# Second half of the value projection moved between the two value-product runs, second half of the key transposes between the two score runs

## The reference

```python
qkv = x @ Wqkv                      # 128 -> 3 * 1024, 16 heads of 64
q = l2norm(q) * qs ; k = l2norm(k) * ksc      # then rotary tables on both
bq, bk, bv = windows of 32 tokens; keys and values of the window and of the one before it
sim = einsum('bhwie,bhwje->bhwij', bq, bk2) * 8
attn = softmax(where(mask, -max, sim))
out = einsum('bhwij,bhwje->bhwie', attn, bv2)
x = out @ Wo + x                    # then the feed-forward
```

## Time and profile before

| | |
|---|---|
| median of three executions | 3936.07 us |
| profiled execution | 3927.86 us, span 3926.1 us |
| TensorE matmul, busy | 94% of the span |
| TensorE weight load, VectorE, GpSimd, ScalarE, busy | 72%, 77%, 66%, 58% |
| mean granted TensorE clock | 0.988 |
| DMA | 48 GB/s mean |

### The profile page before, as it was taken

How to read it: one execution, slowest core, us unless ns; L and a number is a source line. 1 busy time by engine, 2 the same in 40 slices (tenths; PEclk the granted TensorE clock), 3 DMA queues, 4 the chain that set the end, 5 groups by cost and what they waited for, 6 DMA issues and landing times.

```text
span 3926.1 us, 163005 instructions
## 1 busy us (share of the span) xinstructions
PE 3686.9 (94%) x67712; PEld 2840.2 (72%) x67712; DVE 3008.4 (77%) x5061; ACT 2270.5 (58%) x4270; POOL 2597.5 (66%) x3029
## 2 busy tenths in 40 slices
PE   6999979999999999999999999999999999999998
PEld 3555547777767777668877677777677777778876
DVE  7666658878778788778887788877788887888876
ACT  3555546666546666456666466665466664566662
POOL 4545548777548787368887288775478874678870
PEclk8999989999999999999999999999999999999999
DMA  1000012222212222122222122222122221122220
GB/s 44 4 6 4 6 33 68 55 58 60 58 32 60 57 57 59 41 49 60 61 57 56 30 64 56 60 59 60 32 58 56 60 61 41 48 60 60 60 52 22
DMA packets 136307, 189.03 MB, mean 48 GB/s; under 512 B 38006, under 2 KB 58484, under 8 KB 135412
## 3 DMA queue, kind: packets, MB, share of 16 engines
q1 hardware_dynamic: 135540, 178.23, 17.7%
HBM read 22.67 MB, written 2.10 MB: 6 GB/s over the span
## 4 chain that ended last, share of the span: by engine, by line
PE 76%; issue 4%; POOL 3%; DVE 2%; ACT 0%; DMA 0%; POOLq 0%; SPq 0%; DVEq 0%; ACTq 0%
PE PS L1270 18%; PE PS L1417 10%; PE PS L1256 10%; PE PS L1294 8%; PE PS L1280 8%; PE PS L1257 8%; PE PS L1258 8%; PE PS L1476 2%; PE PS L1411 2%; PE PS L1454 1%; PE PS L1447 1%; POOL t L1182 1%; PE PS L1442 1%; POOL t L1187 1%; DVE m L1803 0%
## 5 line engine op out<-in xcount | busy, mean ns | idle before, releaser
L1182 POOL TENSOR_TENSOR t<-t 128x1024 f32<-128x1024 f32 x384 | 908.3, 2370 | 368.2 <-DVE t L1764 366.9
L1187 POOL TENSOR_TENSOR t<-t,rn 128x1024 f32<-128x1024 f32 x384 | 723.6, 1905 | 29.8 <-POOL rn L150 27.3
L1542 ACT ACTIVATE va<-PS 128x512 f32<-128x512 f32 x384 | 229.8, 598 | 631.9 <-PE PS L1258 631.6
L1763 DVE TENSOR_TENSOR t<-PS,rope 128x512 f32<-128x512 f32 x768 | 523.6, 682 | 27.9 <-ACT sq L1577 26.0
L1256 PE MATMUL PS<-w_hi,xh 128*128 128x512 f32 x1152 | 514.7, 447 | 22.8 <-DVE xl L1063 11.3
L1764 DVE TENSOR_TENSOR t<-PS,rope 128x512 f32<-128x512 f32 x768 | 522.9, 681 | 0.0
L1577 ACT ACTIVATE sq<-PS 128x512 f32<-128x512 f32 x768 | 454.2, 593 | 33.0 <-PE PS L1258 17.4
L1270 PE MATMUL PS<-constants,t 128*128 128x128 f32 x3072 | 443.3, 277 | 19.8 <-POOL t L1187 13.2
L1258 PE MATMUL PS<-w_lo,xh 128*128 128x512 f32 x1152 | 458.4, 398 | 0.0
L1257 PE MATMUL PS<-w_hi,xl 128*128 128x512 f32 x1152 | 458.3, 398 | 0.0
L1770 DVE TENSOR_REDUCE ss<-sq 128x16 f32<-128x1024 f32 x384 | 448.5, 1209 | 0.0
(11 more groups left out here) (167 smaller groups left out, 7697.7 us busy)
## 6 DMA issues: line engine op xcount, KB each, us to landing
vs<-va SPq DMA_DIRECT2D x768, 130.0 KB
vs<-va SPq DMA_DIRECT2D x768, 65.0 KB
t<-in_L_ffn_Wqkv SPq DMA_DIRECT2D x18, 512.0 KB, 4.5
w_out<-in_L_ffn_Wo SPq DMA_DIRECT2D x6, 512.0 KB, 3.9
a_normed<-in_L_attn_x SPq DMA_DIRECT2D x8, 256.0 KB, 6.4
a_xo<-in_L_attn_x SPq DMA_DIRECT2D x8, 256.0 KB, 2.9
out<-total SPq DMA_DIRECT2D x8, 256.0 KB, 3.5
w_raw<-in_L_ffn_W SPq DMA_DIRECT2D x6, 341.0 KB
```

The source lines that it names most:

```text
L1182: pool.tensor_tensor(mine[:, i, :], mine[:, i, :], t2[:, i, :], ALU.add).then_inc(done, 1)
L1187: pool.tensor_tensor(h, h, bc(rn[:, H * i:H * (i + 1)], 2, HB), ALU.mult).then_inc(done, 1)
L1763: dve.tensor_tensor(o1, src, bc(rope[:, 2 * i, t, :], 1, 8), ALU.mult)
```

## The change

On TensorE the second half of the value projection now stands between the two value-product runs, behind `turn_q(0)` alone, and goes to bank 5. Before it overwrites bank 5 it waits for the second rotary pair on the keys (`rk_made`). `turn_q(1)` goes behind the second value-product run and into bank 6, for which it waits for the rotary pair on q's first half (`rq_made`). `turn_mixed(1)` writes bank 5 and so waits for the value copy (`v_made`). The next slot's q projection into bank 6 waits for `qT_made` instead of `v_made`. `turn_k(1)` stands between the first score run and the output projection. On ScalarE the value copy goes between the two query copies. The closing slots keep `turn_q(1)` where it was. VectorE, GpSimd and SyncE have the same instructions in the same order.

```diff
+        def q_bank(projecting, c):
+            return 4 if c == 0 else 6 if projecting else 5
...
                 def turn_q(c):
                     pe.wait_ge(qn_made, at(T, 1, 1, 1))
                     if project_new:
-                        pe.wait_ge(rk_made, at(T, 0, 2, c + 1))
-                    turn(4 + c, lambda j: roped(0)(4 * c + j), qt_mm)
+                        if c == 0:
+                            pe.wait_ge(rk_made, at(T, 0, 2, 1))
+                        else:
+                            pe.wait_ge(rq_made, at(T, 0, 2, 1))
+                    turn(q_bank(project_new, c), lambda j: roped(0)(4 * c + j), qt_mm)
...
                 def turn_mixed(c):
                     if score:
                         pe.wait_ge(qT_made, at(T, 1, 2, c + 1))
+                    if project_new and c == 1:
+                        pe.wait_ge(v_made, at(T, 0, 2, 2))
...
                     project(1, 1, 5, t, k_mm)
-                    pe.wait_ge(v_made, at(T, 1, 2, 2))
+                    pe.wait_ge(qT_made, at(T, 2, 2, 2))
                     project(0, 0, 6, t, q_mm)
                 if closing:
-                    pe.wait_ge(v_made, at(T, 1, 2, 2))
+                    pe.wait_ge(qT_made, at(T, 2, 2, 2))
...
                 if score:
                     turn_q(0)
+                if closing:
                     turn_q(1)
+                if project_new:
+                    pe.wait_ge(rk_made, at(T, 0, 2, 2))
+                    project(2, 1, 5, t, v_mm)
                 if mix:
                     mix_half(1)
-                if project_new:
-                    pe.wait_ge(rq_made, at(T, 0, 2, 1))
-                    project(2, 1, 6, t, v_mm)
+                if score and not closing:
+                    turn_q(1)
...
                 if score:
-                    turn_k(1)
                     pe.wait_ge(on_made, at(T, 2, 2, 2))
...
                     score_half(0)
+                    turn_k(1)
...
                 def turned_q(c):
                     act.wait_ge(s_mm, at(T, 2, 1, 1))
                     act.wait_ge(qt_mm, at(T, 1, 2, c + 1))
-                    pairs(qT, c, 4 + c, qT_made)
+                    pairs(qT, c, q_bank(0 in ages, c), qT_made)
...
                     turned_q(0)
+                if 0 in ages:
+                    values(lay, s, t, 1, 5)
+                if 1 in ages:
                     turned_q(1)
-                if 0 in ages:
-                    values(lay, s, t, 1, 6)
-                if 1 in ages:
                     turned_k(0)
```

## The result

The changed kernel takes 3961.88 us in the median of six runs (3952.71 to 3966.03), against 3934.43 us for the kernel before in the same runs (3925.79 to 3943.39). The ratio is 1.0065, 95% interval 1.0046 to 1.0083. Repeated on another chip it was 1.0044 (1.0027 to 1.0062). It is slower, by 17 to 26 us, where 20 us less was forecast and 3952 us was the upper end of the range. The profiled execution took 3966.03 us; the one before took 3927.86 us.

A forecast was written before the change was run, and what follows sets the result against it. TensorE, busy 94% and 76% of the chain, was taken as the bound. Direct terms -26, -20.5 and +5 gave -41 us, the cautious reading -14; -20 was taken: 3936 - 20 = 3916 us, range 3892 to 3952.

The forecast's parts named there:

- a stop: In TensorE's small-matmul runs: end of a 16.4 KB instruction block whose successor has not landed; 1.10 us in one slot.
- (a): First to second value-product run: stretch grows from 1.02 to 1.33 us, winning 26 us, or 20 read cautiously.
- (b): First to second score run: stretch grows from 1.98 to 2.51 us, 3.30 us start to start, winning 20.5 us.
- cautious reading: Whole slot: loss interpolated against stretch length, winning 20 and 11 us, losing 17; sum -14 us.
- The rule behind the step: Between TensorE's runs: about 2.9 to 3.1 us must pass from start to start; a shortage is paid at block ends.
- (c): Second value-product run to first score run: stretch shrinks from 2.96 to 2.17 us, losing 5 us, bounds 0 and 67.
- Rival B: First score run becomes the new place of stops: +67 - 26 - 20.5 = +21 us, 3957 us; chance 0.18.
- Rival A: Stops only move to the first score run, transposes or output projection: 3936 us, 3925 to 3947; chance 0.29.
- (d): TensorE's new waits: keys' rotary pair has 1.0 us to spare, cover for `on` falls from 0.8 to 0.44 us.
- (e): ScalarE: value copy free; key copy ends 0.3 us before TensorE wants it; a sixth of a microsecond lost costs 30 us.
- C: Whole kernel: the full direct sum, -41 us, 3895 us; chance 0.53 together with the forecast.

The follow-up runs named there:

- experiment 4: Kernel before with one added semaphore increment on TensorE in each full slot, which nobody waits for: 1.0023 to the kernel before.
- experiment 3: Kernel before with only `turn_k(1)` moved behind the first score run: 1.0055 to the kernel before, 3967.22 us.
- experiment 8: Kernel before with the value projection's second half ahead of the second value-product run, behind both query transposes: 0.9953 to the kernel before, 3921.39 us.
- experiment 9: As experiment 8, with `turn_k(1)` ahead of the second half of `turn_mixed` in full slots: 0.9883 to the kernel before, 3895.30 us.
- experiment 7: Kernel before with `turn_k(1)` behind the first score run, in opening slots alone or in full slots alone: 1.0018 and 1.0023 to the kernel before.
- e9: Kernel before with `turn_k(1)` behind the first score run in the full slots alone: 1.0023 to the kernel before.
- experiment 2: Changed kernel with `turn_k(1)` back ahead of the masks everywhere, leaving only the value move: 0.9994 to the kernel before, 3943.95 us.
- experiment 5: As experiment 1, with `turn_k(0)` ahead of `turn_q(1)` in full slots, on TensorE and ScalarE: 1.0146 to the kernel before, 3998.61 us.
- experiment 6: Changed kernel and experiment 1's kernel repeated side by side on one chip: 1.0044 and 1.0016 to the kernel before, 3947.30 and 3938.72 us.
- experiment 1: Changed kernel with `turn_k(1)` back ahead of the first score run in opening slots alone: 1.0006 to the kernel before, 3951.01 us.
- run 27: Not a follow-up run: the words say that of 67 us at the first score run, 27 us came.

## Why the prediction was wrong, step by step

**What bounds the kernel, what a stop is.** What bounds it was right. That a stop is the end of a block fits the unchanged number of packets and experiment 4, and stays a reading. Value-product stops fell with the stretch between the runs, in all fourteen profiles: 1.02 us of stretch, 63.3 to 73.7 us of issue in six; 1.28 us, 40.2 to 52.6 in six; 1.75 us, 15.3 and 21.6.

**(a), the value-product runs.** Right in size. Forecast: 1.33 us of stretch, stops near 0.8 us, 80 to 90 of them, 40 us in all. Measured: 1.28 us, 0.71 us in the chain shown, 82 of them, 44.9 us.

**(b), the second score run.** This step failed. "3.30 us is enough" was to save 20.5 us, 11 in the cautious reading. The stretch became 2.38 us as meant, and the score runs' issue went from 11.1 us (7.2 in the other profile) to 15.3 (14.0 in the repetition), of which 13.3 and 13.5 in the second run: 2 to 6 us lost there, none won. With the key move alone (experiment 3) it is 15.7.

The rule behind the step was uneven. The 2.91 us of the value-product runs count the whole stop, 1.10 us; the 3.08 us of the score runs count only the 0.31 us that the view calls issue. The chain of the kernel before has these pieces around it:

```profile
1489.16 0.25 PE PS L1280 x9
...
1489.71 0.78 PE PS L1280 x49
```

That run took 0.25 + 0.31 + 0.78 = 1.34 us, its stop is 0.55 us, and the sum is 0.79 + 1.98 + 0.55 = 3.32 us. Measured alike, the rows gave 2.91 and 3.32 us, no single distance, and 3.30 us had no margin. Nor did the distance decide: with 0.90 + 2.38 = 3.28 us from start to start, 0.04 us short of 3.32, a second score run that stops still loses 0.58 us on average, where it lost 0.49 before (from the start times in the trace).

Why is open. That a shortage from the shortened approach to the first score run is carried on to the second is an inference. Experiments 8 and 9 do not bear it out: with 2.5 and 2.2 us ahead of the first score run and 1.98 us ahead of the second, the issue in the score runs is 1.3 and 6.0 us, less than with longer stretches in experiment 7 (e9), 13.1 us. A run's own stretch is not all that counts.

**(c), the first score run.** The right place, the wrong size: forecast +5 us, with 0 and 67 as bounds. Measured: 12.5 us of new stops in the transposes, and a first score run of 0.90 us in the median instead of 0.79, which at 180 slots is 20 us; the sum of the slot's medians grew by 0.09 us, 15 us. Together about 27 us. With -19 of (a) and +4 for the score runs' issue that gives +12, and the slots of the two profiles differ by 11. The tenth of a microsecond appears only when both moves are made (medians of 0.79 in experiments 2 and 3). The shorter stretch ahead of the run does not make it by itself: it is 2.31 us in the changed kernel and 2.22 us in experiment 9, where the run takes 0.79. It is lost late in the run, at about its 112th instruction by the start times in the trace, and no view names a wait there. This is Rival B's place at less than half its price, in company with Rival A's result for the full slots (nothing won).

**(d), the new waits.** Right. No row shows TensorE waiting for the keys' rotary pair, the value copy or `on` in full slots.

**(e), ScalarE.** The keys' copy ends 0.47 us ahead of the first score run where 0.3 was forecast (0.79 before). I took it first for the cause of the 0.90, and experiment 5 for its test. Experiment 7 speaks against it: in e9 the lead is 0.36 us and the run takes 0.79. That theory fell.

**What was left out.** All steps were worked out for the 180 full slots. The six opening slots go through the same code, without the value products and the output projection that covered `turn_k(1)`'s copy. They cost 0.28% side by side (experiment 6), 0.18% on the kernel before (experiment 7), and 12 to 14 us by the trace of the changed kernel, so 7 to 14 us, and they more than the full slots turn "no change" into "slower": without them the changed kernel stands at 1.0006 and 1.0016. The prediction priced a moved step at every place but the one where its cover does not exist.

**The others' waits.** VectorE's, to set beside the earlier trace rows:

```profile
DVE state L1859 <- PE PS L1429: 221.2, 192, 4.1
DVE rden L1843 <- PE PS L1298: 179.8, 192, 1.9
```

Two waits for TensorE in every slot, as forecast; the second grew from 0.83 to 0.94 us, where 1.1 was said. VectorE sets nothing here either.

**Sum.** By the trace the full slots stand at +12 us where -20 was forecast, which is (b) and (c), and the opening slots add 7 to 14: +19 to +26. The two measurements give +17 and +26. With the full slots known to some 10 us only, this agreement is partly luck. Of the rivals, A holds for the full slots taken alone (experiments 1 and 6), and C came nowhere near. B has the right sign, and its +21 us fits the measurement by luck: of its 67 us at the first score run 27 came, the 20.5 us that it counted as won in the score runs did not, and it knew nothing of the opening slots.

**What stays open.** How much of the loss is the clock's: in the same rounds it is lower with the changed kernel (experiment 6), and about 5 us of the opening slots' loss lie in a low stretch without a wait, but no run holds the clock fixed. What experiment 5's order gives without its wait on `qT_made`. Why the first score run takes 0.90 with both moves. And the places of block ends: experiment 4 shows that they are worth 0.2%, and no experiment holds them fixed while an order changes.

## What to carry to other kernels

Where runs of small instructions outpace the instruction supply, read the stretch between the starts of two runs, and put long instructions between those that stand closest. Whether the stretch that they are taken from can spare them is not read from its length: with 2.3 us left there (and the key transposes moved) the stops came back, with 2.5 and 2.2 us (experiments 8 and 9) they did not. Price a moved step in every variant of the loop body, the first and last iterations above all: there the work that hides it may be absent. Below 0.2 to 0.3%, a single added instruction can do as much as the edit.

## What the runs showed of the hardware that was not expected

A semaphore increment that nobody reads, once a slot, cost 0.23% (0.14 to 0.33). A wait of 2.35 and one of 0.97 us, 0.85 + 0.66 us of work between them, were followed by 8 us at a granted clock of 0.57; in the kernel before, where the waits at that place were 0.84, 0.48 and 0.54 us, the lowest 8 us were at 0.79.
